# Per-group attention weights loaded in quarters, and one weight piece's low part moved down VectorE's order

## The reference, cut to what matters

```
q, k, v = x Wq^T, x Wk^T, x Wv^T          # 32 query heads, 8 key/value heads, 128 wide
q, k    = rope(rmsnorm(q)), rope(rmsnorm(k))
k_all   = concat(cached keys (512, by block table), k)      # 640 keys
scores  = q k_all^T / sqrt(128), masked beyond the cache's length
probs   = softmax(scores)
out     = (probs v_all) Wo^T              # 512 wide
```

## Time and profile before

| | |
|---|---|
| time, median of three runs | 1388.8 us |
| the profiled execution's own time | 1392.05 us |
| its span, first to last instruction | 1390.3 us |
| mean granted TensorE clock | 0.996 of full speed |
| PE matmuls, busy | 1361.8 us (98%) |
| DVE, busy | 1200.7 us (86%) |
| ACT, busy | 870.2 us (63%) |
| POOL, busy | 776.8 us (56%) |
| bytes moved | 80.46 MB, mean 58 GB/s |

### The profile page before, as it was taken

One profiled execution on the slowest core, in us unless ns is written; L12 is line 12 of the kernel. 1 busy time (PEld: TensorE's weight loads), 2 busy tenths in 40 slices (PEclk: granted clock), 3 DMA queues, 4 the chain that ended last, 5 costly groups with the idle time before them and its releaser, 6 DMA issues.

```text
span 1390.3 us, 23385 instructions
## 1 busy us (share of the span) xinstructions
PE 1361.8 (98%) x8007; PEld 1185.8 (85%) x8007; DVE 1200.7 (86%) x2628; ACT 870.2 (63%) x2216; POOL 776.8 (56%) x817
## 2 busy tenths in 40 slices
PE   8899999999999999999999999999999999999998
PEld 6688888888888888888888888888888787878887
DVE  8889898989898989898989898989899978866783
ACT  6677676767676767676767676767777652213221
POOL 7766666666666666666666666666666500111111
PEclk9999999999999999999999999999999999999999
DMA  6110211121111101111211121112121221111212
GB/s 230 57 32 29 80 62 31 32 75 62 31 46 62 62 31 54 54 61 32 72 36 63 32 76 33 62 32 71 31 73 32 107 95 45 46 47 46 77 46 69
DMA packets 27411, 80.46 MB, mean 58 GB/s; under 512 B 9523, under 2 KB 10547, under 8 KB 23955
## 3 DMA queue, kind: packets, MB, share of 16 engines
q1 hardware_dynamic: 10898, 45.29, 9.1%
q0 software_dynamic: 16384, 33.59, 7.7%
HBM read 76.74 MB, written 2.10 MB: 57 GB/s over the span
## 4 chain that ended last, share of the span: by engine, by line
PE 82%; DVE 13%; ACT 2%; issue 2%; DVEq 1%; another core or an unknown queue 0%; POOL 0%; ACTq 0%
PE proj_ps L110 9%; PE proj_ps L112 9%; PE proj_ps L111 9%; PE turn_ps L755 9%; PE score_ps L112 5%; PE value_ps L110 5%; PE value_ps L111 5%; PE value_ps L112 5%; PE score_ps L111 5%; PE score_ps L110 5%; PE gu_ps L110 2%; PE gu_ps L112 2%; PE gu_ps L111 2%; PE turn_ps L717 2%; PE turn_ps L724 2%; DVE probs L1617 2%
## 5 line engine op out<-in xcount | busy, mean ns | idle before, releaser
L548 POOL DMA_INDIRECT kg<-kc,idx x256 | 262.0, 1023 | 277.8 <-issue 263.2
L1210 ACT ACTIVATE probs<-probs,shift,rstd 128x640 f32<-128x640 f32 x256 | 234.4, 918 | 137.6 <-DVE shift L1606 137.5
L558 POOL DMA_INDIRECT vg<-vc,idx x256 | 257.8, 1007 | 70.7 <-issue 70.7
L1642 DVE TENSOR_TENSOR pt_lo<-turn_ps,pt_hi 128x512 fp32r<-128x512 f32 x320 | 217.1, 686 | 43.9 <-ACT pt_hi L1216 29.7
L1617 DVE CUSTOM_DVE_ANT_0 probs<-score_ps,mask 128x640 f32<-128x640 f32 x256 | 209.1, 820 | 44.8 <-PE score_ps L112 40.2
L1216 ACT ACTIVATE pt_hi<-turn_ps 128x512 fp32r<-128x512 f32 x320 | 186.3, 593 | 84.8 <-PE turn_ps L755 73.4
L755 PE MATMUL turn_ps<-cst,probs 128*128 128x128 f32 x1280 | 192.6, 273 | 1.6 <-DVE qt_lo L1594 0.8
L110 PE MATMUL proj_ps<-w_hi,xt_parts 128*128 128x256 f32 (+1 forms) x500 | 190.6, 381 | 1.4 <-issue 1.4
L755 PEld LDWEIGHTS turn_ps<-cst,probs 128*128 128x128 f32 x1280 | 157.8, 141 | 28.2 <-DVE probs L1635 2.2
L112 PE MATMUL proj_ps<-w_hi,xt_parts 128*128 128x256 f32 (+1 forms) x500 | 169.7, 339 | 0.0
L111 PE MATMUL proj_ps<-w_lo,xt_parts 128*128 128x256 f32 (+1 forms) x500 | 168.7, 337 | 0.0
(11 more groups left out here) (240 smaller groups left out, 3273.4 us busy)
## 6 DMA issues: line engine op xcount, KB each, us to landing
w_raw<-wqkv SPq DMA_DIRECT2D x7, 1536.0 KB
wo_raw<-wo SPq DMA_DIRECT2D x8, 1024.0 KB
wa_sb<-wa SPq DMA_DIRECT2D x7, 1024.0 KB, 4.8
kg<-kc,idx POOLq DMA_INDIRECT x256
vg<-vc,idx POOLq DMA_INDIRECT x256
wg_raw<-wg SPq DMA_DIRECT2D x2, 1376.0 KB
wu_raw<-wu SPq DMA_DIRECT2D x1, 2752.0 KB
wd_raw<-wd SPq DMA_DIRECT2D x1, 2560.0 KB, 12.4
```

What stands on the lines that cost most here:

```text
L548: pool.indirect_dma_start(kg[:, b % 2, c, :], None, kc, bass.IndirectOffsetOnAxis(ap=idx[:, s // B % 2, b * NC + c:b * NC + c + 1], axis=0))\
L558: pool.indirect_dma_start(vg[:, b % 2, c, :], None, vc, bass.IndirectOffsetOnAxis(ap=idx[:, s // B % 2, b * NC + c:b * NC + c + 1], axis=0))\
L1210: act.activation(row, row, ACT.Exp, bias=shift[:, h:h + 1], scale=rstd[:, b % 2, h:h + 1], accum_out=sums[:, h:h + 1])\
L1642: dve.tensor_tensor(pt_lo[:, at, :], turn_ps[1 - j % 2][:, :], pt_hi[:, at, :].bitcast(F32), ALU.subtract).then_inc(p_lo_done[j], 1)
```

## The change

The loads of both weights are cut into quarters, one DMA each. A quarter k of group g's `w_raw` is issued once the key and value projection of step 8(g-1) + k has been done, and a quarter h of `wo_raw` once that of step 8(g-1) + 4 + h has been done. The first group's `wo_raw` is loaded in four DMAs one behind the other. The waits on `w_in` and `wo_in` count four DMAs for each load. In `step_with_last_w` on DVE the low part of weight piece 2 moves from ahead of the first two normalised heads to behind the low part of turned probabilities 3 (the fourth).

```diff
-                    sp.dma_start(wo_raw[:, :, :], wo[0]).then_inc(wo_in, 16)
+                    for h in range(REP):
+                        sp.dma_start(wo_raw[:, h, :], wo[0, :, h, :]).then_inc(wo_in, 16)
                     sp.dma_start(x_raw[:, FIRST:B, :, :], xt_b[:, FIRST:B, :, :]).then_inc(x_in[2], 16)
                     for g in range(1, HK):
                         for n in range(len(W_PIECES)):
                             sp.wait_ge(w_lo_done[n], g)
-                        sp.dma_start(w_raw[:, :, :], wqkv[g]).then_inc(w_in, 16)
+                        for k in range(NK):
+                            sp.wait_ge(kv_projected, (g - 1) * B + k + 1)
+                            sp.dma_start(w_raw[:, k, :], wqkv[g, :, k, :]).then_inc(w_in, 16)
                         for n in range(len(WO_HALVES)):
                             sp.wait_ge(wo_lo_done[n], g)
-                        sp.dma_start(wo_raw[:, :, :], wo[g]).then_inc(wo_in, 16)
+                        for h in range(REP):
+                            sp.wait_ge(kv_projected, (g - 1) * B + NK + h + 1)
+                            sp.dma_start(wo_raw[:, h, :], wo[g, :, h, :]).then_inc(wo_in, 16)
...
-                            wait(act, w_in, g * 16)
+                            wait(act, w_in, g * (NK * 16))
...
-                        wait(act, wo_in, (g + 1) * 16)
+                        wait(act, wo_in, (g + 1) * (REP * 16))
...
                         split_probs(s, b, 1)
                         split_probs(s, b, 2)
-                        split_w(g + 1, 2)
                         normalise(s + 1, b1, (0, 1))
                         split_probs(s, b, 3)
+                        split_w(g + 1, 2)
                         normalise(s + 1, b1, (2,))
                         split_probs(s, b, 4)
                         rotate_k(s + 2, b2)
```

## The result

The changed kernel takes 1397.2 us (median of 4 runs, 1396.11 to 1399.4) against 1389.51 us for the kernel before in the 4 runs beside it (1388.67 to 1390.33): 1.0049 times as long, 95% interval [1.0034, 1.0065], so 4.7 to 9.0 us slower. Forecast were 1396.7 us and 7.9 us.

A forecast was written before the change was run, and what follows sets the result against it. PE, busy 98%, was taken as the bound, waiting for VectorE's low parts. Losses of 6 x 1.15 + 0.97 = 7.9 us, quarters at 0, on the 1388.8 us median gave 1396.7 us; 8-in-10 range 1394.0 to 1399.0.

The forecast's parts named there:

- What bounds the kernel: Whole kernel: PE, busy 98%, has no idle time left to give back and waits for low parts on VectorE.
- The gap before the reciprocal is filled for free: VectorE, step with b = 5: the low part's 1.15 us cost nothing before, as the reciprocal waits for the last exponential anyway.
- Two turns of PE wait, one behind the other: Step with b = 5: the queries' turn starts 0.99 us late, then the new key's turn is late by the whole 1.15 us.
- all others are unchanged: Sign: only the L730-to-L730 step around the new wait gets 1.1 us longer; every other step keeps its length.
- The size: 1.15 us in six steps, 0.97 in one: Seven steps that split the piece: 1.15 us lost in each of six, 0.97 in group 0, 7.9 us in all.
- the stretch stays: First two multiplies, groups 1 to 6: they still take 1.45 us after the change, so the sum is 7.9 us.
- the rival with 6.8 us: Whole load stretched the two multiplies; quartered, low part 3 starts 0.19 us earlier in 6 steps: 6.8 us, 1395.6; chance 0.13.
- 0.80 us: Lower bound per step with b = 5, set by ACT's high part 3 ending at 966.60: seven steps make 5.6 us.
- The quarters cost nothing: Quartered loads on SP: 42 more issues and 3 at the start, all hidden, priced at 0 us.
- The quarters cost as well: Rival: shifted gathers and VectorE instructions meet oftener, 3 to 4 us more, 1400 us; chance 0.06.
- the move is free: Rival: PE's two turns aren't tied to VectorE, or the engine doesn't run the list's order; 1388.8 us unchanged; chance 0.04.
- faster: Rival: whole loads cost more than waits show; quarters freeing all 10.2 us of PEld's waits give 1386.5 us; chance 0.03.

The follow-up runs named there:

- e6: Changed kernel with the moved low part in two halves, the first back in the gap before the reciprocal: 1394.76 us, 1.0021 of the kernel before.
- e1: Quartered loads alone, VectorE's order as in the kernel before: 1392.71 us against 1391.23, ratio 1.0002.
- e3: Changed kernel with the moved low part one place further up, ahead of the low part of turned probabilities 3: 1397.1 us, ratio 1.0045.
- e7: Changed kernel with the key rotation moved into the gap ahead of the first two multiplies: 1396.84 us, 1.0039 of the kernel before.
- e2: Kernel before with only the low part moved, whole loads kept: 1397.66 us, ratio 1.0048.
- e10: Changed kernel measured once more, unchanged, beside the kernel before: 1397.66 us against 1390.36, ratio 1.0051.
- e4: Kernel before, but in the step with b = 4 heads are multiplied between the low parts and piece 0 is split later: 1395.8 us, ratio 1.0032.
- e5: e4 with piece 0's low part given to GpSimd and two of four key gathers put behind the norms: 1393.03 us, 1.0014 of the kernel before.
- e8: e5 with two of four key gathers behind the norms in the step with b = 5 too: 1397.62 us, 1.0052 of the kernel before.

## Why the prediction was right, and where a size was off

**What bounds the kernel.** Right. PE has no idle time in which a late VectorE could be made good: the 0.96 us or so of each group are in the sum of the 60 steps (6.64 us) and aren't given back later.

**The gap before the reciprocal is filled for free.** Right, 1.06 us of idle time after the change, and shown from both sides: out of the gap altogether the low part costs 0.96 us, half out 0.40 us (e6), back in 0 (e1), and behind the gap its place makes little difference (e3). That it must be this work, queued ahead of low part 4, is e7.

**Two turns of PE wait, one behind the other.** Right. PE waits before L729 7 times (forecast 6 or 7), 0.64 us by its own row, and PEld 1.08 us. PE's row is smaller than the lateness because the durations shown of the matmuls ahead reach into the wait: counted from the new key's turn before, the queries' turn starts at 972.69 - 956.24 = 16.45 us and not at 968.78 - 953.15 = 15.63, so it is 0.82 us late where 0.99 were forecast. PEld's wait for the cached keys' low part stays, 3.9 us against 3.2. Of the signs named, "all others are unchanged" misses by 0.06 us, the distance behind that step.

**The size: 1.15 us in six steps, 0.97 in one.** This is the term that was mis-sized. Measured are 0.90 to 0.99 us in the seven groups (0.97 in group 0, as forecast), 6.64 us for 7.9 forecast. The failing step is the last weighing of the prediction: "the stretch stays". It does not. From the start of the reciprocal to low part 3 there are 966.81 - 965.24 = 1.57 us before and 969.74 - 968.35 = 1.39 us after: low part 3 comes 0.18 us earlier, and 1.15 - 0.18 = 0.97. The cause is not the one that the rival with 6.8 us named, though that rival's sum fits. It blamed the load, and e1 and e2 show that it has no part: without a whole load the multiplies keep 1.45 us, with one and the low part moved they take 1.23. (In group 6 no load of `w_raw` is left to be issued at that moment anyway, which the prediction overlooked.) What runs beside them decides:

- before, the low part (964.09 to 965.31) still runs when the gather starts at 964.97, for 0.34 us; the gather takes 1.16 us, to 966.13, and the pair of multiplies 1.45
- e7, the rotation's last instruction overlaps the gather by 0.18 us (969.06 - 968.88): 1.00 and 1.29 us
- after, e2, e3 and e6, in group 6, nothing runs on VectorE when the gather starts: 0.94 to 0.95 and 1.23 to 1.24 us

The ends of these instructions show how. The gather ends 0.82 us behind the subtraction's end, before (966.13 and 965.31) and in e7 (969.88 and 969.06); alone it takes 0.95. And the first multiply ends 0.31 to 0.32 us behind the gather's end: before it takes 0.99 us, to 966.44, after 0.77 us, to 969.33 (the gather ends at 969.02), in e7 0.84 us, to 970.20.

The twelve traces hold many more such pairs between 60 and 1100 us. All 113 gathers that were issued while a `w_lo` subtraction had still 0.14 to 1.01 us to run end 0.81 to 0.84 us behind it. All 642 multiplies of this form that start 0.29 to 0.53 us before the end of a gather end 0.31 to 0.32 us behind it, and take 0.60 to 0.84 us. The gather doesn't stretch every multiply that runs beside it: the 63 that start 0.69 us or more before its end, and the 149 that start under 0.25 us before it, take 0.54 to 0.59 us. The place of the first multiply before the change, 0.67 to 0.68 us, lies at the edge: of 46 that start 0.66 to 0.68 us before a gather's end, 12 are stretched (this very multiply, in groups 1 to 6 of the kernel before and of e1) and 34 are not. That is how group 0 escapes: there the gather is held longest (1.74 us, to 139.49), but the multiply starts 0.70 us before its end and takes 0.55.

So a subtraction that reads two operands from SBUF holds up the gather, and the gather holds up a multiply that starts in a certain stretch ahead of its end. The move takes away its own 0.2 us of stretch; without that the 1.15 us would stand. A still shorter pair would not have made the step cheaper, as low part 3 starts right behind ScalarE's high part 3: at 969.74, with the high part ending at 969.11 + 0.60 = 969.71, and so in group 1 of e2 with a pair of 1.02 us. This is the bound that the prediction used for its 0.80 us and for the rival's 0.19.

The Trainium skill, SBUF — State Buffer, section "Who interferes with whom", says that transfers don't contend with a compute engine, and e1 agrees; it also says that a VectorE instruction with two SBUF inputs contends with a GpSimd instruction that reads SBUF. I had used only its sentence on multiplies, and so took the gather's 1.16 us as fixed. The same section infers that such a subtraction leaves descriptor generation for a gather alone; the gather's 1.16 us against 0.95 speak against that here. And by the sentence on multiplies whoever issues first keeps the ports for its whole instruction, where here a multiply is held only in a part of the gather's time.

**By the profile alone 6.6 us, by the medians 7.7.** The interval of the ratio (4.7 to 9.0 us) holds both, and e10's and e2's (5.1 to 9.0 and 5.0 to 8.3 us) too. What the other 1.1 us between the two figures are isn't shown. That the forecast of 1396.7 lies so near the median of 1397.2 is thus partly luck: with the right term it would have been 1388.8 + 6.6 = 1395.4.

**The quarters cost nothing.** Right, 1.0002 [0.9991, 1.0012] in e1. An issue on SP takes 0.33 us there, 0.43 at the start, and from 60 us on ScalarE never waits for `w_raw` or `wo_raw`. The Trainium skill, DMA: Bandwidth & Descriptors, section "Anatomy of one DMA — SWDGE (gpsimd) path", has about 2.0 us of fixed time for a transfer. It has it for those that GpSimd issues, and the prediction's estimate of 90 us took it for SP's; here the page of the profile reads 3.2 us from issue to landing for a quarter of `w_raw`, and all of it is hidden.

**The rivals.** "The quarters cost as well", "the move is free" and "faster" are each excluded: the first by e1 (at most 0.12%, 1.7 us), the second by e2, the third by both.

## What to carry to other kernels

A full-looking engine may have a gap where it waits for another, and the work that fills it is free only there: moved out, it costs its length less what it did to its neighbours, and one place more or less behind the gap changes little. So read the idle time in front of the instruction that waits, not the engine's share, and ask of any filler whether it stands ahead of what the bounding engine waits for. Cutting transfers that are already hidden, or removing one of several waits on a full engine, moved nothing here: in e4 and e5 the wait came back one or two steps later.

## What the runs showed of the hardware that I had not expected

- VectorE and GpSimd hold each other up in a chain. A gather issued beside a `w_lo` subtraction (two SBUF operands) ends 0.81 to 0.84 us behind it (113 of 113), and a multiply that starts 0.29 to 0.53 us before a gather's end ends 0.31 to 0.32 us behind that end (642 of 642). So 0.34 us of overlap make the gather 1.16 us instead of 0.95, and the pair of multiplies 1.45 instead of 1.23.
- Two subtractions with SBUF operands didn't run side by side. VectorE's of 128x1024, started 0.48 us behind the first of GpSimd's two, took 2.38 us instead of 1.22 and ended 1.14 us behind the second (e4). The other way round, in the kernel before, GpSimd's of 128x512 started 0.61 us behind VectorE's of piece 1 and took 1.77 us instead of 1.30. On GpSimd itself 128x1024 take 2.39 us (e5).
- ScalarE stood for 2.08 us before one high part with no releaser in the trace, in six groups of one kernel (e8) and in no other. It is unexplained.
